# Fused last stage: the gathers of expert rows issued behind the normalising and the output bias, once the step's scores are through

## What is computed

```python
out = jnp.einsum('te,etd->td', gates, ys)                 # two experts' rows for each row, weighted
...
f = jnp.einsum('bhqd,bhkd->bhqk', fq, fk) / jnp.sqrt(jnp.float32(ATTN))
f = f + jnp.where(mask == 0, jnp.float32(-1000000000.0), jnp.float32(0.0))
ps = jax.nn.softmax(f, axis=-1)
attns = jnp.einsum('bhqk,bhkd->bhqd', ps, fv)
...
return attns @ out_w.T + out_b
...
h = bit_linear(x, w1); h = depthwise_conv1d(...); h = jax.nn.silu(h); return bit_linear(h, w2)
x = x + jnp.tanh(g_xattn[1]) * _L1_xattn_ref(_layernorm(x, axis=-1), ctx_1024, ctx_1024, ...)
x = x + jnp.tanh(g_ffn[1]) * _L1_ffn_ref(_layernorm(x, axis=-1), ...)
```

## Time and profile before

| | |
|---|---|
| time before, median of 3 runs | 1648.94 us (1635.04 to 1659.93) |
| the profiled execution's own time | 1640.07 us |
| its span | 1637.7 us |
| mean granted clock of TensorE | 0.955 |
| busy share: PE / weight loads / DVE / ACT / POOL | 92% / 76% / 72% / 61% / 42% |
| the last stage | from about 740 us to the end |

### The profile page before, as it was taken

How to read it: one execution, slowest core, us unless ns; L and a number is a source line. 1 busy time by engine, 2 the same in 40 slices (tenths; PEclk the granted TensorE clock), 3 DMA queues, 4 the chain that set the end, 5 groups by cost and what they waited for, 6 DMA issues and landing times.

```text
span 1637.7 us, 51409 instructions
## 1 busy us (share of the span) xinstructions
PE 1505.6 (92%) x20222; PEld 1246.3 (76%) x20222; DVE 1174.8 (72%) x3120; ACT 995.8 (61%) x2018; POOL 692.5 (42%) x611
## 2 busy tenths in 40 slices
PE   5999999999839999997899999999999999999988
PEld 2777777777729999986677777777787878888864
DVE  5788878876544222234587989889898899888875
ACT  3787777766214444443456566766666667767756
POOL 2234667575441111144565454444444444333320
PEclk9899999987559999998999999999999999999999
DMA  9999950000038888861000000000000000000000
GB/s 299 393 387 386 382 196 24 24 31 21 27 113 257 263 267 262 255 196 39 26 23 18 18 17 22 24 22 22 23 23 22 22 22 22 12 16 12 14 9 23
DMA packets 97661, 173.36 MB, mean 106 GB/s; under 512 B 12320, under 2 KB 44960, under 8 KB 97168
## 3 DMA queue, kind: packets, MB, share of 16 engines
q1 hardware_dynamic: 84816, 144.05, 26.3%
q0 software_dynamic: 11600, 25.65, 4.6%
q10 hardware_dynamic: 1008, 0.40, 0.1%
HBM read 79.41 MB, written 90.64 MB: 104 GB/s over the span
## 4 chain that ended last, share of the span: by engine, by line
PE 39%; DVE 8%; issue 4%; ACT 1%; POOL 1%; another core or an unknown queue 0%; DVEq 0%; ACTq 0%
PE L1psY L1283 6%; PE L1psY L1290 6%; PE L1psM L1332 5%; PE L1psY L1275 5%; PE L1psT L1324 4%; PE L1psS L1301 4%; PE L1psT L1310 2%; DVE L1sc L1708 1%; PE L1psF L1380 1%; PE L1psF L1361 1%; PE L1psF L1398 1%; DVE L1den L1719 1%; DVE L1am L1770 1%; PE L1psM L1390 1%; DVE x L1600 1%
## 5 line engine op out<-in xcount | busy, mean ns | idle before, releaser
L1851 POOL TENSOR_TENSOR L1sc<-L1sc,L1top 128x1024 f32<-128x1024 f32 x64 | 121.8, 1904 | 240.8 <-DVE L1top L1715 240.8
L1463 ACT ACTIVATE L1KT<-L1psY 128x512 f32<-128x512 f32 x128 | 78.0, 609 | 226.7 <-PE L1psY L1275 216.9
L1004 ACT ACTIVATE GhT<-GpsH,Gwx 128x256 f32<-128x256 f32 (+1 forms) x312 | 117.9, 445 | 149.9 <-PE GpsH L972 143.6
L855 POOL TENSOR_TENSOR L0sc<-L0sc,L0top 128x1024 f32<-128x1024 f32 x64 | 121.6, 1900 | 178.6 <-DVE L0top L564 177.7
L1856 POOL TENSOR_TENSOR L1sc<-L1sc,L1rden 128x1024 f32<-128x1024 f32 x64 | 121.8, 1904 | 177.0 <-DVE L1rden L1724 177.0
L1283 PE MATMUL L1psY<-L1xnT,L1WQ 128*128 128x128 f32 x1024 | 142.8, 283 | 1.0 <-ACT L1xnT L1458 1.0
L1021 DVE TENSOR_TENSOR yg<-GpsY,Gwx 128x256 f32<-128x256 f32 (+1 forms) x78 | 30.3, 389 | 158.0 <-PE GpsY L980 84.9
L861 POOL DMA_INDIRECT rows_in<-L0xr,slot x128 | 124.5, 972 | 45.3 <-issue 31.8
L1275 PE MATMUL L1psY<-cx,L1WK 128*128 128x128 f32 x1024 | 138.4, 279 | 2.6 <-DVE L1identh L1791 2.5
L980 PE MATMUL GpsY<-Gwx,GhT 128*128 128x128 f32 x1080 | 133.1, 275 | 0.0
L980 PEld LDWEIGHTS GpsY<-Gwx,GhT 128*128 128x128 f32 x1080 | 130.9, 192 | 2.7
(11 more groups left out here) (326 smaller groups left out, 3732.4 us busy)
## 6 DMA issues: line engine op xcount, KB each, us to landing
Gwx<-in_experts SPq DMA_DIRECT2D x78, 579.0 KB, 4.3
rows_in<-L0zero SPq DMA_DIRECT2D x1, 33792.0 KB, 92.7
rows_out<-L0zero SPq DMA_DIRECT2D x1, 33792.0 KB
Gxg<-rows_in SPq DMA_DIRECT2D x57, 128.0 KB, 3.8
rows_out<-yg POOLq DMA_DIRECT2D x57, 128.0 KB
cx<-in_ctxT SPq DMA_DIRECT2D x64, 64.0 KB
out<-X SPq DMA_DIRECT2D x64, 64.0 KB, 1.7
L0ctxT<-in_ctxT SPq DMA_DIRECT2D x1, 2560.0 KB, 18.6
```

The source lines that it names most:

```text
L855: nc.gpsimd.tensor_tensor(sc[:, t % 4, :, :], sc[:, t % 4, :, :], top[:, t % 2, :].unsqueeze(2).broadcast_to([P, H, S]), ALU.subtract).the ...
L1004: nc.scalar.activation(hT[:, u, m, 0:blocks(t) * P], psH[:, u, m, 0:blocks(t) * P], ACT.Gelu, bias=wx[:, w, ob1 + m:ob1 + m + 1]).then_inc ...
L1851: nc.gpsimd.tensor_tensor(sc[:, t % SR, :, :], sc[:, t % SR, :, :], broad(top[:, t % 2, :]), ALU.subtract).then_inc(s["shifted"], 1)
```

## The change

In steps 6 and later the fetch on POOL moves from the head of the step to behind `normalise` and `add_bo`, ahead of `shift`, and waits for `scores_ps` of this step's scores (`k - LX + 1` = `k`: tile `k - 1`, whose scores PE makes in step `k`). Steps 0 to 5 are as they were.

```diff
             for k in range(LAST):
                 tx, tv = tile(k, LX), tile(k, LV)
-                if k >= 6:
-                    for t in fetches.get(k, []):
-                        fetch(t)
                 if tv is not None:
                     normalise(tv)
                 if k < 6:
@@ -1881,6 +1878,10 @@
                         fetch(t)
                 if tile(k, LN) is not None:
                     add_bo(k)
+                if k >= 6:
+                    for t in fetches.get(k, []):
+                        pool.wait_ge(s["scores_ps"], k - LX + 1)
+                        fetch(t)
                 if tx is not None:
                     shift(tx)
```

## The result

The change takes 1626.17 us in the median of 20 runs (1608.75 to 1640.69); the kernel before, run beside it, 1642.24 (1631.51 to 1665.07). The ratio is 0.9886, interval 0.9859 to 0.9913: a gain of 1.1%, 18.7 us by the ratio, against the 19.0 of the sum. (The ratio is formed from the fast runs of both kernels, the medians from all.) The profiled execution of the changed kernel took 1622.12 us (span 1619.7, mean clock 0.957), against 1640.07 (1637.7, 0.955).

What follows compares the result with a forecast made beforehand. PE was taken to lose 32.7 us in `values` to POOL's gather issues, with DVE as co-bound. Gains of 10.9, 5.1 and 3.0 us made 19.0, so 1640.07 became 1621; between bases 1621 and 1630 the forecast was 1625, range 1605 to 1645.

Steps and rivals of the forecast that it cites:

- stall of `values`: PE's block `values` loses time in 33 of 43 steps with a moved fetch; 32.7 us, upper bound of the gain.
- eight steps: A window of eight steps with gathers, 105.28 us before the change, was to take about 102.5.
- The hold by POOL's issue: While POOL writes a gather's descriptors, PE gets few new instructions; `values` runs dry, 0.93 us in the step examined.
- Rival 3: The gathers do not hold PE; the gap in `values` has another cause in PE's program; 1640 us, chance 0.05.
- DVE as the cover: PE's stall partly covered DVE's `collect` and norm work; eight steps gain 2.8 us, the rest becoming a wait for `add_x`.
- Lateness up to 0.77 is free: DVE's `residual` may come up to 0.77 us late without cost; each us beyond costs one.
- Rival 1: The whole stall in `values` comes back as gain, 32.7 us: 1607 us, or 1616 from the median; chance 0.12.
- No new stall behind the scores: Gathers issued behind the scores cost PE 0; upper bound the old price, 0.93 us in each of 44 steps.
- rival 2: The stall moves: a block behind the scores starves, 0.93 us lost in all 44 steps; 1640 to 1649 us, chance 0.10.
- `shift`: On POOL behind the gathers, it waits for `tops` anyway; cost 0, bounds 0 and 0.7 us in one step of four.
- Landing: Gathers land 4.3 us behind the scores' end, before DVE's `collect` starts at 4.7; cost 0, margin 0.4 us.
- rival 4: Gathers land late and DVE's `collect` waits; gain gone at 3.7 us after issue, 1677 us at 4.6; chance 0.06.

Runs made afterwards that it cites:

- e4: The kernel before with the gathers of steps 6 and later waiting for the first half of `project_v`, so the second issue falls on the scores; ratio 1.0311.
- e2: The kernel before without the second gather from tile 20 on, the remaining one issued in the old place; ratio 0.9834.
- e3: The changed kernel plus two plain 64 KB loads a step, issued by SP at about the gathers' old place; ratio 0.9892.
- e1: The changed kernel without its wait for `scores_ps`, so the gathers start as soon as POOL is free; ratio to the kernel before 1.0219.
- e6: The changed kernel with DVE's 25 feed-forward pieces dealt 9, 8, 2 and 6 over four steps; ratio to the kernel before 0.9959.
- e5: The kernel before with DVE's 25 feed-forward pieces dealt 9, 8, 2 and 6 over four steps instead of three; ratio 0.9972.
- e11: The changed kernel with DVE's pieces dealt 12, 6, 4 and 3, the last three at their step's start; 1616.78 us, ratio to the kernel before 0.9736.
- e12: The kernel before with plain 64 KB copies issued by POOL instead of the indirect gathers for tiles 20 to 63; ratio 1.001.
- e9: The kernel before, unchanged, run again on another chip; stage 744.04 us, median on that chip 1660.23 us.
- e8: The kernel before with the gathers of steps 6 and later waiting for the second half of the queries, onto `project_v`; 1628.62 us, a single execution.

## Why the prediction was right, point by point

The time (1625 forecast, 1626.17 measured) came out by the steps that were given. That it came out to 1 us is partly luck: 1625 lies between two bases, 1621 and 1630, of a kernel whose median moved from 1648.94 to 1642.24 when it was run again. The ratio says more: 19.0 of 1640.07 us is 0.9884, measured was 0.9886. The terms can be compared one by one, as stage time gained between the two profiled executions:

| term | predicted | measured |
|---|---|---|
| stall of `values` | 32.7 us, gone | 32.8 to 0.1 |
| steps 7 to 10 | 5.1 | 5.12 |
| steps 11 to 18 | 3.0 | 2.40 |
| steps 19 to 49 | 10.9 | 11.73 |
| behind them | 0 | −0.08 |
| sum | 19.0 | 19.16 |
| eight steps | 102.5 | 102.09 |

Behind step 64 the changed kernel's profiled execution took 1.39 us longer (with 3.41 us at a granted clock of 0.50 from 1573.2 us on, which the kernel before did not have there), so the spans differ by 18.0.

- **The hold by POOL's issue.** Right on the chips that have it. e4 moves it onto the scores with the same delay (1.53 us), e2 removes it by halving the gathers, e3 excludes the bytes. Rival 3 falls there; on chip B it describes what is seen, but the rule that it calls on is shown by no run. That PE is short of new instructions remains a reading: the runs show when it is held and not what it lacks. That PE lives on what is queued, that blocks of large matmuls are spared by that, and that POOL writes descriptors during the issue, were my assumptions and were not shown.
- **DVE as the cover.** Right. Forecast steps were 12.3, 13.1, 13.4, 12.07, 12.3, 13.8, 13.4, 12.06; measured from 1036.99 on 12.26, 13.08, 13.39, 12.06, 12.25, 13.61, 13.38, 12.06. The one that is off is the heaviest, 0.2 us quicker: from `residual` to `residual` DVE takes 13.61 us there instead of the 13.82 of the earlier trace rows. The difference lies in two instructions, L1702 and L1741: they ran beside the second issue in the kernel before (0.57 and 0.90 us) and take 0.35 and 0.69 in the changed one. "Lateness up to 0.77 is free" held to the hundredth: `residual` 0.96 us behind the scores' end cost 0.19 (12.26 − 12.07). Rival 1 falls with it. What the cover turned into I had only half right: about half of the 13.5 us shows at `turn_x`, which waits for `add_x`; 2.2 show behind `turn_back` and the rest is spread over other blocks, most of it in the steps where DVE binds.
- **No new stall behind the scores: the conclusion held, its reason did not.** I took 0 from the earlier trace rows and put the gathers at S + 0.1, as though any place behind the scores were safe. They run from S + 0.37, and e1 shows that 0.3 to 0.5 us earlier the place costs 2.3 us or more in every fourth step, and earlier still 1.9 in another. I gave the wait no value of its own; without it the move loses 2.2% instead of gaining 1.1 (e1). The chance of rival 2 (0.10) stood for a block starving behind the scores. The danger was real, though it lay at their end and ahead of it, and with the issues there the kernel is slower than before by 2.2% (e1) and 3.1% (e4), and not by 0 to 1%. What makes 0.37 us behind the scores safe and 0.04 not is open.
- **`shift`.** Cost 0 was right: it waits for `tops` 37 times, 32.8 us in total, so in 37 of the 44 steps the issues in front of it still leave slack (before: 45 times, 180.2 us).
- **Landing.** The sign that I had given for rival 4 came: DVE waits for a gather ten times, 9.7 us in total, where the kernel before has no such wait from step 7 on. Nine of the ten fall in steps 7 to 16: the gathers start later than I put them, and the margin of 0.4 us was gone there. The rival's price did not come: steps 7 to 10 gained their 5.1 us all the same, and the stage its 19.2. Steps 11 to 18 gained 0.6 us less than forecast, and these waits may be in that. In the first steps of the kernel before `collect` was slow beside `shift` (L1600 takes 1.69 us from 867.40 on, with `shift` on POOL from 867.04 to 868.94; the shortest L1600 takes 0.33).
- **One effect not foreseen, without cost.** Where the first issue starts while DVE's L1765 runs, it lasts longer, 1.14 to 1.26 us in 12 steps. DVE and POOL of the changed kernel:

```profile
1109.63 0.94 DVE L1765 SCALAR_TENSOR_TENSOR L1hs<-L1hs,L1hc 128x512 f32<-128x512 f32 x1
...
1110.17 1.25 POOL L1866 DMA_INDIRECT yr<-rows_out,slot  x1
...
1113.37 1.91 POOL L1851 TENSOR_TENSOR L1sc<-L1sc,L1top 128x1024 f32<-128x1024 f32 x1 [0.69 <-DVE L1top L1715]
```

The first issue takes 1.25 us instead of 0.98 while DVE's L1765 takes 0.94 instead of 0.68; `shift` still waits for `tops`.

What the prediction had no word for is the chip. Its 19 us are those of a chip that shows the hold. The unchanged changed kernel was not run on B or D; e6 against e5 (0.9959 and 0.9972) says that there the move is worth nothing that can be measured.

## What to carry to other kernels

When a dense block of small matmuls shows a gap that ends in "issue", look at what POOL was issuing at that time. If its DMA issues lie there, move them by a semaphore of the matrix engine to a place behind the last dense block and behind the signal that others wait for; here, put there without the wait, they cost more than where they were. Before costing the removal of a stall at its full length, take the next engine's work from step to step: here two fifths of it was cover, and dealing that engine's work anew gave the rest of it back (13.6 us, e11). And measure such an effect on more than one chip.

## What the runs showed of the hardware that I had not expected

- The hold of PE while POOL issues an indirect DMA is seen on chips A (scores 2.16 us in e1, 2.72 in e4) and C (`values` 1.89 to 2.16 us in three late steps of four, e9) and in the execution of the earlier trace rows, and not on B (1.09 us with the same overlap, e5) and D (1.10 us for scores under an indirect issue, e12). The kernel before takes 1656 to 1660 us on the first two and 1585 to 1590 on B and D. What makes the chips differ is open.
- The hold reaches further than the instructions of a dense block: in the e1 step of 1112.52 both DVE and ACT, waiting for two different blocks of PE, were freed 2.9 us after `project` began, 1.65 us after the second issue began.
- The granted clock fell to 0.50 for 3.41 us in five of the eight steps of e1 in which PE sat idle for 1.4 to 2.7 us, and in two steps of e4; in the other three of e1 it stayed at 1.00. In the one of them shown above `project_out` took 3.11 us instead of 1.95.
- The issue itself can take longer beside DVE's work: 1.14 to 1.26 us instead of 0.98 in the 12 steps of the changed kernel in which it starts while L1765 runs, and up to 1.5 us in e6.
- In e8 a DVE instruction of 0.16 us took 2.56 us beside POOL's L1856 of 1.91 us.
